# Layer 1's experts in a four-layer transformer kernel: from all experts for every token to routed blocks

## The chip, the cores and the metric

The kernel runs on one core of a Trainium2 chip. The metric is the device time of one execution in microseconds. Before the change the median of 3 runs is 2787.91 us (2787.64 to 2787.95). All matrix work is done by TensorE (PE in the profile); VectorE (DVE), ScalarE (ACT) and GpSimd (POOL) work on data in SBUF; TensorE's results stand in eight PSUM banks, which VectorE and ScalarE empty. The queue of SyncE (SP) issues almost all transfers.

## The reference, cut to what matters

The input is 16 sequences of 256 tokens, each a row of 128 numbers: 4096 tokens in 32 tiles of 128, or 8 chunks of 512. Four layers follow on each other. Each has an attention and a feed-forward part, whose results are scaled by gates (and whose inputs are normalized, scaled and shifted) by numbers that come from a conditioning vector through a SiLU. Layer 1's feed-forward part is itself a small transformer layer over groups of tokens, and its second half is the mixture of experts that the change is about:

```python
x1 = _ln(src + _attention(src, ...), ln1_g, ln1_b)      # 16 heads of 8
gates = softmax(xf @ gW + gb)                           # 8 experts
top2_scores, top2_idx = top_k(gates, 2)
w = (one_hot(top2_idx, 8) * top2_scores[..., None]).sum(1)
h = relu(einsum('nd,edf->enf', xf, W1) + b1[:, None, :])    # d 128, f 256
y = einsum('enf,efd->end', h, W2) + b2[:, None, :]
out = _ln(x1 + einsum('ne,end->nd', w, y), ln2_g, ln2_b)
```

Each token uses two of eight experts, with the softmax weights of all eight (not renormalized over the two). The result is multiplied by the layer's gate and added to the residual stream. Layer 0 has a mixture of experts of the same shape (8 experts, 2 per token, with two up products and a SiLU); layer 2 has 16 experts, layer 3 none. Layer 2's attention has 16 heads of 8 and is causal.

## The kernel before

**Stages.** The program is a list of nine stages: the wide attention of layer 0, its routed experts, the wide attention of layer 1, `narrow_attention(1)` (the attention inside layer 1's feed-forward part), `moe(1, 8)` (its experts), `narrow_attention(2)` (layer 2's attention), `moe(2, 16)`, and the two stages of layer 3. Each stage is written as a loop of ticks. Every engine has its own stream of instructions, written out by hand tick by tick and executed strictly in order; semaphores join the streams. A stage may lend its last ticks to the stage behind it: the `Guest` that a stage gives as its `start` is run there, from tick `guests_at` on, and a stage's last pieces (its tail) are run in the first ticks of the next stage. There is no planner: the place of a piece in the loop of ticks is its place in each queue.

**Layer 1's narrow attention** has 128 ticks of 1.9 us and a drain to tick 137. In a tick TensorE computes one pair of heads' scores twice, once as they are and once transposed, and the value product of an earlier tick. VectorE takes the row maxima of the scores from PSUM (`rowmax`, line 3015). GpSimd turns each group of them into two bf16 parts (`negate`, lines 2738 and 2740), TensorE transposes these (line 2965) and adds them to the transposed scores, and ScalarE exponentiates. For each of 16 pairs of tiles (8 ticks each) GpSimd also splits the queries and keys into three bf16 parts (`Parts.gpsimd`, lines 2664 to 2672), SP stores them to device memory (line 2686) and loads them back in the layout that the products want (line 2695). Before the change the stage's last 11 ticks host the first pieces of `moe(1, 8)` (`guests_at` is 126).

**Layer 1's experts**, `moe(1, 8)`, compute every expert for every token: 8 chunks of 512 tokens with 8 experts each are 64 steps. A step has two up products, weights of 128x128 by 512 tokens, two ReLUs on ScalarE, and a down part of eight 128x128 products; VectorE weights each expert's four result tiles by the token's gate and adds them to an accumulator (`vector_down`, line 2359). The gates come from TensorE's logits, ScalarE's exponential and VectorE's choice of two by comparison of all pairs (line 1153 and those behind it). When a chunk's eight experts are in, its own normalization follows (`gpsimd_finish`, lines 2488 to 2498, and its counterparts on VectorE): add to x1, statistics, a power on GpSimd (line 189), scale and shift, gate, add to the residual X (`gated`, `added`).

**Layer 0's routed experts** are the model for the change. Two of its chunks are computed densely, in the time in which the other six, 3072 tokens and so 6144 token-expert pairs, are routed. VectorE finds each token's two experts with `max` (line 1525) and `max_index` (line 1529); TensorE ranks the tokens within their expert with products of a mask; VectorE makes from that a table that assigns experts to 31 blocks of 256 rows (lines 1579 to 1587 and on). GpSimd scatters each tile's rows twice, once for each expert, to a buffer `hs` in device memory (line 1854, 48 indirect transfers). Then come 31 blocks: SP loads the block's rows (line 1891) and its expert's weights (line 1898), TensorE turns the rows (line 1432), computes the up and the down part on 256 rows, VectorE adds the second bias (line 1706) into one of two result buffers, and SP stores it to `ys` (line 1903). Their result is brought together during the wide attention of layer 1: GpSimd gathers a tile's two result rows (`late_fetch`, line 1209, two indirect transfers per tile of 128 tokens) and weights and adds them itself (`late_combine`).

**Layer 2's narrow attention** has the same ticks as layer 1's, with a causal mask. Its first step for a pair of tiles is the normalization of X for the chunk that the pair belongs to: `stats0` and `stats1` on VectorE, `normed0` and `normed1`, and `turn` on TensorE. These need the chunks of X that layer 1's experts have finished; the last chunk of the experts finishes in the first ticks, as the tail of the stage before.

## Time and profile before

| | |
|---|---|
| median of 3 runs | 2787.91 us |
| the profiled execution's own time | 2784.46 us |
| its span | 2782.7 us |
| mean granted TensorE clock | 0.984 |
| TensorE busy | 2608.1 us, 94% |
| VectorE busy | 2015.3 us, 72% |
| ScalarE busy | 1664.5 us, 60% |
| GpSimd busy | 1180.9 us, 42% |
| device memory traffic | 87 GB/s over the span |

The span is the time from the first to the last instruction that the profiler recorded; the execution's own time holds 1.8 us more. Times in rows are microseconds from the start of the span. The stretches that the change touches are: layer 1's narrow attention with ticks from about 1510, its tick 122 at 1742 and its drain to 1771; layer 1's experts from 1771 to 2031; layer 2's narrow attention, tick 0 at 2031, to about 2250 and on. Layer 0's blocks run from 777 to 889. A granted clock of 1.00 is TensorE's full clock of 2.4 GHz, 0.50 its lower level of 1.2 GHz.

### The profile page before, as it was taken

What the parts mean: (1) busy time and instruction counts of PE and PEld (TensorE: products, weight loads), DVE (VectorE), ACT (ScalarE), POOL (GpSimd) and SP (SyncE); (2) the same over time, 40 slices, a digit from 0 to 9 for tenths busy, and PEclk for the clock granted to TensorE, in tenths of its full rate; (3) what the DMA queues carried; (4) which work ended last, traced back from release to release, by engine and by line L of the source; (5) the groups of instructions that cost most, each with busy time, mean ns of one, the idle gap of its engine ahead of it and who ended that gap; (6) DMA issues with size and microseconds to landing.
All of it is one profiled execution on the core that took longest, in us unless ns stands there. A gap on an engine that the chain in (4) does not pass through costs nothing.

```text
span 2782.7 us, 67999 instructions
## 1 busy us (share of the span) xinstructions
PE 2608.1 (94%) x24870; PEld 1786.5 (64%) x24870; DVE 2015.3 (72%) x5620; ACT 1664.5 (60%) x4107; POOL 1180.9 (42%) x1620
## 2 busy tenths in 40 slices
PE   5999999998989999999997999999989988999898
PEld 2666666665677666666665555677767765666666
DVE  6888888876544666666666998556678886887675
ACT  3888888884334777677765777534335544434665
POOL 6888888862611566211113454122333321014441
PEclk9999999999999999999999999999989999999999
DMA  3022222112275122111113544000054433435750
GB/s 113 17 54 76 76 75 53 62 37 75 98 224 164 30 45 46 32 33 32 32 32 106 182 142 133 1 1 17 13 159 141 129 102 63 93 78 154 208 164 28
DMA packets 218858, 230.81 MB, mean 83 GB/s; under 512 B 18609, under 2 KB 188273, under 8 KB 216481
## 3 DMA queue, kind: packets, MB, share of 16 engines
q1 hardware_dynamic: 212000, 207.58, 26.9%
q10 hardware_dynamic: 3456, 12.58, 1.4%
q0 software_dynamic: 3072, 6.30, 0.8%
q8 instruction: 201, 3.29, 0.5%
q14 instruction: 129, 1.05, 0.1%
HBM read 165.87 MB, written 75.60 MB: 87 GB/s over the span
## 4 chain that ended last, share of the span: by engine, by line
PE 71%; DVE 13%; ACT 7%; issue 4%; POOL 2%; SPq 1%; DMA 1%; ACTq 0%; another core or an unknown queue 0%; DVEq 0%; POOLq 0%
PE pb L163 63%; ACT big L967 4%; PE pb L663 3%; ACT big L160 2%; DVE big L3015 2%; DVE big L837 2%; PE pb L596 1%; DVE big L236 1%; PE pb L2986 1%; SPq L2686 1%; DVE big L3520 1%; PE pb L249 1%; DVE big L820 1%; DVE big L179 1%; DVE big L842 1%
## 5 line engine op out<-in xcount | busy, mean ns | idle before, releaser
L163 PE MATMUL pb<-big 128*128 128x128 f32 (+12 forms) x19624 | 2344.0, 326 | 100.1 <-ACT big L160 32.6
L163 PEld LDWEIGHTS pb<-big 64*128 64x128 bf16 (+4 forms) x19624 | 1475.6, 143 | 756.5 <-issue 424.7
L160 ACT ACTIVATE big<-pb 128x512 f32<-128x512 f32 (+7 forms) x1481 | 846.1, 620 | 552.7 <-PE pb L163 292.6
L160 ACT ACTIVATE big<-pb,big 128x512 f32<-128x512 f32 (+2 forms) x502 | 276.3, 585 | 426.7 <-PE pb L163 360.1
L3015 DVE TENSOR_REDUCE big<-pb 128x4 f32<-128x1024 f32 (+1 forms) x256 | 277.6, 1086 | 69.5 <-PE pb L163 64.9
L967 ACT ACTIVATE big<-big 128x256 f32<-128x256 f32 x512 | 253.7, 499 | 65.8 <-DVE big L842 64.6
L967 ACT ACTIVATE big<-pb,big 128x128 f32<-128x128 f32 (+1 forms) x512 | 256.7, 526 | 60.0 <-DVE big L822 59.8
L837 DVE CUSTOM_DVE_ANT_0 big<-pb,big 128x256 f32<-128x256 f32 x512 | 186.7, 422 | 96.7 <-PE pb L163 93.5
L187 POOL TENSOR_SCALAR big<-big 128x4 f32<-128x4 f32 (+2 forms) x102 | 26.7, 262 | 535.6 <-DVE big L182 535.4
L174 POOL TENSOR_TENSOR big<-big 128x128 f32<-128x128 f32 x168 | 74.5, 457 | 348.8 <-DVE big L171 348.7
L1046 POOL TENSOR_TENSOR big<-big 128x512 f32<-128x512 f32 x128 | 159.7, 1273 | 140.7 <-DMA big<-recip 140.7
L663 PEld LDWEIGHTS pb<-big 64*128 64x128 f32 x3584 | 146.2, 139 | 75.0 <-ACT big L967 58.4
L663 PE MATMUL pb<-big 64*128 64x64 f32 x3584 | 158.3, 225 | 26.0 <-ACT big L967 25.0
L1020 POOL TENSOR_TENSOR big<-big 128x32 f32<-128x32 f32 x32 | 174.1, 5440 | 2.7
L747 DVE TENSOR_TENSOR big<-pb,big 128x512 f32<-128x512 f32 x256 | 164.0, 681 | 12.2 <-PE pb L163 10.9
L904 DVE COPY big<-pb 128x384 f32<-128x384 f32 (+1 forms) x256 | 157.3, 615 | 5.2 <-PE pb L663 4.3
L2359 DVE SCALAR_TENSOR_TENSOR big<-pb,big 128x128 f32<-128x128 f32 x256 | 72.0, 344 | 95.6 <-PE pb L163 95.6
L1011 POOL TENSOR_TENSOR big<-big 128x256 f32<-128x256 f32 x128 | 82.3, 643 | 86.0 <-DVE big L747 82.9
L596 PEld LDWEIGHTS pb<-big 128*128 128x128 f32 x512 | 63.6, 142 | 75.9 <-issue 66.1
L967 ACT ACTIVATION_READ_ACCUMULATOR big<-pb,big 128x1 f32 x512 | 111.1, 217 | 0.0
L236 DVE TENSOR_SCALAR big<-big 128x128 f32<-128x128 f32 x244 | 95.6, 444 | 8.5 <-POOL big L189 8.4
L2738 POOL CAST big<-big 128x16 bf16<-128x16 f32 x96 | 21.8, 227 | 188.2 <-DVE big L3019 73.5
(211 smaller groups left out, 2451.2 us busy)
## 6 DMA issues: line engine op xcount, KB each, us to landing
parts<-big SPq DMA_DIRECT2D x384, 96.0 KB, 2.5
big<-parts SPq DMA_DIRECT2D x72, 512.0 KB, 4.1
big<-recip SPq DMA_DIRECT2D x128, 256.0 KB, 5.3
big<-comb SPq DMA_DIRECT2D x32, 512.0 KB, 8.4
hs<-in_zero SPq DMA_DIRECT2D x10, 1472.0 KB, 8.8
big<-in_wx SPq DMA_DIRECT2D x31, 450.0 KB
parts<-big SPq DMA_DIRECT2D x192, 64.0 KB, 2.1
big<-parts ACTq DMA_DIRECT2D x24, 512.0 KB, 4.6
```

The lines of the kernel that those rows point to most:

```text
L160: return e.activation(o, i, f, bias=bias, scale=scale)
L163: return e.matmul(o, l, r_, start=start, stop=stop, skip_group_check=True)
L236: t = e.tensor_scalar(XN[:, i, :], X[:, self.tiles(c)[i], :], mv[:, k0 + i, 0:1], rs[:, k0 + i:k0 + i + 1], ALU.subtract, ALU.mult)
L596: t = e.transpose(bk[:, 128 * m:128 * m + 128], QR[(8 * b + n) % 12][:, 128 * m:128 * m + 128], IDF)
L663: t = e.transpose(banks[2 * (p % 2) + half][:, 64 * at:64 * at + 64], PS[p % 2][rows, i, 128 * blk:128 * blk + 128], IDF[rows, rows])
L747: t = e.tensor_tensor(h3(D), h3(bk), TAB[:, 2 * qk + kk, tile, :].unsqueeze(1).to_broadcast([128, 8, 64]), ALU.mult)
L837: t = e.tensor_tensor_reduce(ps[:, i, x], banks[2 * (p % 2) + i][:, x], U[:, 2 * j + i, 128 - 128 * qt:384 - 128 * qt], 1.0, -3.0e38, ALU. ...
L904: e.tensor_copy(*turned_out(t - 1, 0)).then_inc(even_out, 1)
L967: t = e.activation(ps, banks[2 * s + i][:, at:at + w] if causal else ps, ACT.Exp, bias=NM[s][:, m:m + 1], scale=rstd_q(b)[:, qt, h:h + 1] ...
L1020: e.tensor_tensor(half, half, HALF, ALU.pow).then_inc(rms_made, 1)
L1046: e.tensor_tensor(OT[k % 6], OT[k % 6], R[:, 2 * i:2 * i + 2, :], ALU.mult).then_inc(chunk_scaled, 1)
L3015: e.tensor_reduce(m[:, :, 0:n, jj], two[:, :, 0:width].rearrange("p e (q x) -> p e q x", q=n), AXX, ALU.max, negate=True).then_inc(maxed, 1)
```

## The change

`moe(1, 8)` is replaced by a new stage, `routed_ffn()`.

**Routing.** Six of the eight chunks (0 to 5) are routed. Their `turn` (transposition of x1), `logits`, `max0`, `max1`, `route`, `rank`, `place` and the three pieces of the table are hosted in layer 1's narrow attention, whose `guests_at` goes from 126 to 34; one tick there has at most one or two of them. GpSimd scatters from tick 58 on: one indirect transfer a tick in ticks 58 to 73 and 90 to 105, two a tick from 122 to 129.

**Blocks.** The new stage begins with 31 blocks of 256 rows, one a tick, with one up product of 256 columns for each half of f, a ReLU for each half, and a down part of eight 128x128 products (two halves of f for two tiles of rows, each product issued as two instructions). Weights are 128 x 642 f32 a block (329 KB), rows 128 x 256 f32 (131 KB), results the same.

**Dense.** Chunks 6 and 7 are computed as before, 16 steps, behind the blocks. Their logits, gates and first accumulator values are made beside the blocks, as are the shares (softmax weights) and the places of the result rows (`home`) of the routed ones, and the modulation numbers of the next layer.

**Combination.** The 24 routed tiles' result rows are gathered by GpSimd in 12 groups m of two tiles, four indirect transfers each, into three buffers `CHOSEN1`. VectorE, not GpSimd as in layer 0, weights them and adds them to x1, eight operations for a chunk of four tiles, and makes the statistics; GpSimd makes the scale, ScalarE normalizes, and GpSimd does the rest with 256-wide operations and issues the next gathers in the same piece of its order. Chunks 0 and 1 are brought together at ticks TB+4, TB+5 and TB+9, TB+10 (TB is 31, where the dense steps begin); chunks 2 to 5 in the ticks 0 to 3, 10 to 13, 26 to 29 and 42 to 45 of layer 2's narrow attention.

**Layer 2's narrow attention** waits for the routed chunks by a semaphore of their own (`arrived`), takes its statistics one to three ticks later (offsets 5 and 6 in place of 2 and 4), opens with 9 hosted steps in place of 7, and the transfer of the second gates goes from pair 5 to pair 11. The semaphores that engines use to wait for themselves are one per engine in place of one per stage. The host lays out the layer's weights once more, by expert (`wx1`).

```diff
@@ narrow_attention
-            guests_at = 126 if k == 1 else 98
+            guests_at = 34 if k == 1 else 98
...
-                                                           ((2, "stats0"), (4, "stats1"))) if at == i]
+                                                           (((5, "stats0"), (6, "stats1")) if causal else ((2, "stats0"), (4, "stats1")))) if at == i]
...
+            def late_at(t):
+                found = []
+                for c in range(2, 6) if causal else ():
+                    first = 16 * (c - 2) - (6 if c > 2 else 0)
+                    found += [(c, p) for p, at in (("scale", 0), ("sum", 1), ("stats", 2), ("norm", 3)) if first + at == t]
+                return found
...
+                        for c, p in late_at(t):
+                            if p == "norm":
+                                late_ffn_finish(e, c)
@@ the stages
-                 moe(1, 8, X1A.rearrange("p (t c) -> p t c", c=128)), narrow_attention(2), moe(2, 16), layer3_attention(), layer3_mix()]
+                 routed_ffn(), narrow_attention(2), moe(2, 16), layer3_attention(), layer3_mix()]
@@ new functions
+        def late_ffn_fetch(e, m):
...
+            if m >= 3:
+                e.wait_ge(ffn_added, m - 2)
+            for k in range(2):
+                for i in range(2):
...
+                    e.indirect_dma_start(out=CHOSEN1[m % 3][:, k, i, :], out_offset=None, in_=dr["ys"],
+                                         in_offset=bass.IndirectOffsetOnAxis(ap=at, axis=0)).then_inc(chosen_in[m % 3], 16)
...
+        def late_ffn_vector(e, c):
...
+            for a, t in tiles:
+                x = e.scalar_tensor_tensor(out=a[:, 0, :], in0=a[:, 0, :], scalar=SHARE1[:, 0, t:t + 1], in1=X1[:, t, :],
+                                           op0=ALU.mult, op1=ALU.add)
...
+            for a, t in tiles:
+                x = e.scalar_tensor_tensor(out=a[:, 0, :], in0=a[:, 1, :], scalar=SHARE1[:, 1, t:t + 1], in1=a[:, 0, :],
+                                           op0=ALU.mult, op1=ALU.add)
...
+        def late_ffn_finish(e, c):
+            own = gpsimd_own
+            e.wait_ge(ffn_mean, c + 1)
...
+            e.tensor_tensor(LRS, LRS, EPS[:, 0:4], ALU.pow).then_inc(own.sem, own.up())
+            e.wait_ge(own.sem, own.n)
+            e.tensor_tensor(LNMR, LNMR, LRS, ALU.mult).then_inc(ffn_rstd, 1)
+            e.wait_ge(ffn_normed, c + 1)
...
+            for m in (2 * c, 2 * c + 1):
+                a = CHOSEN1[m % 3][:, 0]
+                for b, op in ((two(LNW[:, 256:384]), ALU.mult), (two(LNW[:, 384:512]), ALU.add), (two(GA[:, m, 128:256]), ALU.mult)):
+                    e.tensor_tensor(a, a, b, op).then_inc(own.sem, own.up())
+                    e.wait_ge(own.sem, own.n)
+                e.tensor_tensor(X[:, 2 * m:2 * m + 2, :], X[:, 2 * m:2 * m + 2, :], a, ALU.add).then_inc(ffn_added, 1)
+            for m in (2 * c + 3, 2 * c + 4):
+                if m < 12:
+                    late_ffn_fetch(e, m)
@@ routed_ffn
+            FIRST_TICK = 34
+            def hosted_at(t):
+                found = []
+                for c in ROUTED:
+                    b = 16 * c + FIRST_TICK
+                    found += [(c, p) for p, at in (("turn", 0), ("logits", 2), ("max0", 3), ("max1", 4)) if b + at == t]
+                    if c % 2:
+                        found += [("ABC"[c // 2], p) for p, at in (("route", 5), ("rank", 6), ("place", 6)) if b + at == t]
+                        if c == 5:
+                            found += [("C", p) for p, at in (("table_a", 7), ("table_b", 8), ("table_c", 9)) if b + at == t]
+                return found
...
+            def tensor_block_up(e, j):
...
+                for f in range(2):
+                    t = mm(e, bk[:, 256 * f:256 * f + 256], WB[J % 4][:, 128 * f:128 * f + 128], HTB[J % 3], True, True)
...
+            def vector_block_down(e, j):
...
+                e.wait_ge(y_stored[J % 2], 16 * (J // 2))
+                e.tensor_tensor(YB[J % 2], bk[:, 0:256].rearrange("p (k c) -> p k c", k=2),
+                                WB[J % 4][:, 514:642].unsqueeze(1).to_broadcast([128, 2, 128]), ALU.add).then_inc(y.free, 1)
...
+            def gpsimd(e):
+                for t in range(T + 2):
...
+                    if t == TB + 1:
+                        for m in range(3):
+                            late_ffn_fetch(e, m)
+                    if late_at(t):
+                        late_ffn_gpsimd(e, *late_at(t))
+                    if t >= TB + 9:
+                        gpsimd_finish(e, *finish_at(t))
...
+                    if j + 3 < TB:
+                        sync_rows(e, j + 3)
+                    if 1 <= j and j + 3 < TB:
+                        sync_weights(e, j + 3)
+                    if j >= 1:
+                        sync_store(e, j - 1)
```

## Rows read from the trace of the kernel before

**Rows 1.** The page: busy time, chain by engine, one costly group.

```profile
PE 2608.1 (94%) x24870; PEld 1786.5 (64%) x24870; DVE 2015.3 (72%) x5620; ACT 1664.5 (60%) x4107; POOL 1180.9 (42%) x1620
...
PE 71%; DVE 13%; ACT 7%; issue 4%; POOL 2%; SPq 1%; DMA 1%; ACTq 0%; another core or an unknown queue 0%; DVEq 0%; POOLq 0%
...
L1011 POOL TENSOR_TENSOR big<-big 128x256 f32<-128x256 f32 x128 | 82.3, 643 | 86.0 <-DVE big L747 82.9
```

**Rows 2.** Stretches: us, busy PE, PEld, DVE, ACT, POOL, clock, DMA share, GB/s.

```profile
1550.00:1740.00 190.00, 184.42 (x2202) 101.53 (x2196) 174.93 (x344) 135.96 (x185) 97.61 (x208) 1.00 0.46 142
1740.00:1771.00 31.00, 26.68 (x309) 14.71 (x306) 19.42 (x48) 19.73 (x27) 8.97 (x25) 1.00 0.00 1
1771.00:2031.00 260.00, 257.25 (x1526) 191.35 (x1524) 153.63 (x538) 98.62 (x151) 62.49 (x105) 0.99 0.06 17
2031.00:2053.00 22.00, 15.17 (x148) 9.27 (x150) 17.36 (x43) 2.82 (x4) 12.34 (x22) 0.69 0.38 118
2053.00:2250.00 197.00, 193.11 (x3022) 141.10 (x3020) 159.17 (x321) 107.85 (x169) 68.63 (x130) 1.00 0.47 143
```

**Rows 3.** Waits, 1550 to 1740: who waited for whom, us, times, longest.

```profile
PEld pb L163 <- DVE big L3015: 30.1, 75, 1.0
...
DVE big L3015 <- PE pb L163: 7.1, 20, 0.6
```

**Rows 4.** TensorE's groups by shape, 1780 to 2000: count, busy us, mean ns.

```profile
L163 PE MATMUL pb<-big 128*128 128x128 f32 x907 | 110.5, 275 | 0.0
L163 PE MATMUL pb<-big 128*128 128x512 f32 x224 | 106.7, 599 | 0.0
```

**Rows 5.** Timeline of a layer-0 block: start, duration, instruction, idle before.

```profile
844.09 0.84 ACT L160 ACTIVATE big<-pb,big 128x256 f32<-128x256 f32 x2 [1.37 <-PE pb L163]
...
844.50 0.43 SPq L1903 DMA_DIRECT2D ys<-big  x1
...
844.75 0.38 PE L1432 MATMUL pb<-big 128*128 128x128 f32 x2
...
845.17 0.39 ACT L160 ACTIVATE big<-pb 128x256 f32<-128x256 f32 x1 [0.24 <-PE pb L1432]
...
846.06 0.43 DVE L1706 TENSOR_TENSOR big<-pb,big 128x256 f32<-128x256 f32 x1 [0.18 <-PE pb L163]
...
847.59 0.38 PE L1432 MATMUL pb<-big 128*128 128x128 f32 x2
```

**Rows 6.** A stretch of layer-0 blocks, columns as in rows 2.

```profile
846.00:856.00 10.00, 10.00 (x63) 9.02 (x62) 4.33 (x10) 4.23 (x11) 0.00 (x0) 1.00 0.92 250
```

**Rows 7.** Transfers by kind: count, KB each, median us from issue to landing.

```profile
ys<-big SPq DMA_DIRECT2D x31, 128.0 KB, 4.3
```

**Rows 8.** Timeline of GpSimd, two gathers of layer 0's result rows.

```profile
893.80 0.95 POOL L1209 DMA_INDIRECT big<-ys,big  x1 [0.30 <-issue]
895.07 0.94 POOL L1209 DMA_INDIRECT big<-ys,big  x1 [0.30 <-issue]
```

**Rows 9.** GpSimd's groups by shape, 1780 to 2040: the power.

```profile
L189 POOL TENSOR_TENSOR big<-big 128x4 f32<-128x4 f32 x10 | 10.5, 1050 | 0.8
```

**Rows 10.** Timeline of VectorE, routing pieces of layer 0.

```profile
651.66 0.36 DVE L1525 MAX8 big<-big 128x8 f32<-128x8 f32 x4
...
652.55 0.16 DVE L1529 FIND_INDEX8 big<-big 128x8 uint32<-128x8 f32 x1
...
752.59 0.22 DVE L1587 TENSOR_REDUCE big<-big 128x8 f32<-128x64 f32 x1
```

**Rows 11.** Timeline of TensorE, start of layer 2's narrow attention.

```profile
2042.38 0.40 PE L2965 MATMUL pb<-big 128*128 128x128 bf16 x2 [1.14 <-POOL big L2740]
```

**Rows 12.** A stretch soon after that opening, columns as in rows 2.

```profile
2044.00:2048.00 4.00, 1.96 (x20) 1.43 (x20) 3.00 (x6) 0.00 (x0) 3.63 (x7) 0.50 0.05 14
```

**Rows 13.** VectorE's groups by shape, 1780 to 2000: two comparisons of gates.

```profile
L1155 DVE TENSOR_TENSOR big<-big 128x256 f32<-128x256 f32 x7 | 8.3, 1189 | 0.0
...
L1153 DVE TENSOR_TENSOR big<-big 128x256 f32<-128x256 f32 x7 | 3.0, 427 | 0.2
```

More of the change, by code:

```diff
@@ L1196, in program @@
         NBLK, SLOT_ROWS = 31, 3072
+        place(21632)
+        HOME1 = [alloc(16).bitcast(U32) for _ in range(3)]
+        SHARE1 = alloc(48).rearrange("p (k m) -> p k m", k=2)
+        CHOSEN1 = [WA[:, a:a + 512].rearrange("p (k i c) -> p k i c", k=2, i=2) for a in (2176, 2688, 3200)]
+        LST = WA[:, 3840:3864].rearrange("p (i s) -> p i s", i=4)
+        LMV = WA[:, 3864:3872].rearrange("p (i s) -> p i s", i=4)
+        LRS, LNMR = WA[:, 3872:3876], WA[:, 3876:3880]
         def late_fetch(e, n):
@@ L1238, in routed_experts @@
             T = TD + NBLK
-            own, own_g = moe_own
-            scattered, marked, spaced, share_exped = sem("scattered"), sem("marked"), sem("spaced"), sem("share_exped")
-            placed, table_made = sem("placed"), sem("table_made")
-            rows_in = [sem(f"rows_in{i}") for i in range(3)]
-            weights_in = [sem(f"weights_in{i}") for i in range(4)]
+            own, own_g = vector_own, gpsimd_own
             some = lambda n: [alloc(512) for _ in range(n)]
@@ L2751, in narrow_attention @@
             place(stack_top)
-            own, own_g = narrow_own
+            own, own_g = vector_own, gpsimd_own
             causal = k == 2
@@ L3281, in tail_do @@
                 return go
-            start = Guest(15 if k == 1 else 7, lambda i: [take_piece(b, piece, BK[6:8]) for b, piece in hosted_step(i)],
+            start = Guest(15 if k == 1 else 9, lambda i: [take_piece(b, piece, BK[6:8]) for b, piece in hosted_step(i)],
                           tensor_hosted, vector_hosted, scalar_hosted, gpsimd_hosted, sync_hosted)
@@ L3314, in layer3_attention @@
             place(20480)
-            own, own_g = narrow_own
+            own, own_g = vector_own, gpsimd_own
             bi = WI[:, 512:643]
```

677 lines of the change are left out of this document (658 added, 19 removed).

## The prediction

> **What bounds the kernel now.** I read the page first: TensorE is busy for 94% of the span and holds 71% of the chain that ended last [rows 1]. The table by stretches then cuts out the part that the change touches [rows 2]. Four things are to be seen there. In layer 1's dense experts (1771 to 2031 us) TensorE is busy 257 of 260 us, VectorE 154, GpSimd 62: TensorE alone bounds it. In layer 1's attention (1550 to 1740) VectorE is busy 175 of 190 us. Its waits [rows 3] say that TensorE waited 30.1 us for VectorE's row maxima, and VectorE only 7.1 us for TensorE: VectorE bounds this stage, though TensorE looks busy. In layer 2's attention (2053 to 2250) TensorE leads again, VectorE has 19% free and GpSimd 65%. And the first 22 us of that stage are a stretch of waits, at a mean granted clock of 0.69.
>
> **Part 1, the dense stage that goes: minus 260 us.** 64 expert steps of two 128x512 products and eight 128x128 ones; the rows show 224 and 907 instructions in 220 us, so each product is two instructions [rows 4]. By shares of that stretch a step takes about 3.44 us and a chunk 31 us with gates.
>
> **Part 2, the 31 blocks: 86 us.** Layer 0's blocks in this trace are the model; one lasts 2.84 us (847.59 less 844.75) [rows 5]. A layer-1 block has one up product fewer: 4 instructions of 0.213 us (0.85), a down part of 8 by 0.107 (0.86) and the row turn 0.22, so TensorE wants 1.93 us. ScalarE gives more: the block's activations start 0.25 us after the up part, take 0.84, and the copy of the next rows, queued behind them, 0.39, before the next up part may start: 0.85 + 0.25 + 0.84 + 0.39 + 0.1 = 2.43 us. DMA: weights 329 KB, rows 131, results 131 make 591 KB a block; at layer 0's 250 GB/s [rows 6] that is 2.36 us. The result buffers close a third loop: writing a result (0.43), 0.85 us until SP has issued the weights before it and then the store, landing 4.3 us in the median [rows 7], two buffers. With 132 KB less ahead of the store I take 3.8 us: (0.43 + 0.85 + 3.8) / 2 = 2.55 us. Ends: 2.43 and 2.95 us; I take 2.55, 79 us in all. Beside them: two table loads for Silu, the 1 MB gate broadcast, two gates of about 3.6 us on VectorE, two chunks' turns: 7 us (3 to 14). At the start, the last 16 scatters are queued two a tick from tick 122 of the attention: 16 x 1.26 us [rows 8] and 5 us of other GpSimd work end some 25 us later, the drain of the attention takes 29; scatter landing, row load and copy leave 2 us of TensorE waiting (0 to 8).
>
> **Part 3, the dense rest and GpSimd's queue: 85 us.** Two chunks cost an up part beside the last block's down part (2.6), an up part (1.7), 14 steps of 3.44 and two down parts (3.4), 56 us, and the first pieces of layer 2's attention 5: 61 us if nothing waits. But the gathers are issued here: four for two tiles, 1.26 us each (893.80 to 895.07) [rows 8], 24 tiles, so 60 us of GpSimd for all 48 in place of nothing. Count from the first dense up part. The last result lands and GpSimd starts at 6; twelve gathers end at 21. VectorE weights and adds (eight operations at a 0.28 us pitch, statistics 1.3: 3.8 us) by 22; GpSimd's scale needs 1.6 with the power of 1.05 [rows 9], ScalarE 1.7, GpSimd's eight 128x256 operations at 0.64 [rows 1] 5.8 us: 31; then, in the same piece of its order, eight gathers, 41. Chunk 1's turn repeats it to 64. Only behind that stands the scale of the first dense chunk (65), for which VectorE waits at tick 42 with evacuations behind it; VectorE's normalization also came late, so TensorE's turn at tick 42 waits 8 us. TensorE's next piece, v of pair 0, needs a bank that VectorE empties at about 72. I get 16 us more there, and a late split and return trip of pair 0, so that the next stage starts at 85 in place of 61. Ends: 61, if the order costs nothing, and 97.
>
> **Part 4, routing in layer 1's attention: plus 24 us.** Per pair of chunks VectorE gets eight MAX8 and eight index searches, whose pitch in the timeline is 0.09 and 0.13 us (the first MAX8 of a half at 651.66, its last index search at 652.55) [rows 10]: 2.4 us in four halves; route 1.3, place 1.0, logits 0.3; three pairs are 15 us, the three table pieces 3.4 (some thirteen operations at a pitch of 0.26, such as the one at 752.59) [rows 10]: 18.4 us. An engine that is late by nothing for most ticks pays this in full. TensorE's logits and rank products delay its next scores by some 7 us more; 2 us of VectorE's idle time absorb part. I take 24. Ends: 9, if all 8% of idle time is used, and 38. Scatters there are 1.26 us a tick on a GpSimd at half load [rows 2, 8]; with negated maxima due three ticks later I count nothing for them, 4 us if that cover is gone.
>
> **Part 5, layer 2's attention: plus 52 us.** Here each late chunk stops three engines in turn. VectorE's 3.8 us stand between two row maxima; ScalarE's normalization waits in order for GpSimd's scale, and the exponentials behind it wait: 4.3 us a chunk. Then GpSimd has 5.8 us of arithmetic and up to eight gathers (10.1 us) before the split of the next pair (3.5) and the next negated maxima, for which TensorE waits within three ticks (6 us). For chunk 2 (tick 3) this meets the opening: before, TensorE got its first negated maxima at 2042.38 [rows 11], 11.4 us after tick 0 at 2031; now the dense rest's scaling (14 us), 1.6 + 1.7 + 5.8 and 10.1 put it at 33.7: plus 22. Chunk 3: split and maxima end 28.5 us after its tick, needed at 18.2: 10 + 4.3 = 15. Chunk 4 has four gathers: 5 + 4.3 = 10. Chunk 5 none: 5. Sum 52. Ends: 17 (only the 4.3 us each) and 72: TensorE's clock stood at 0.50, its lower level of 1.2 GHz, at 2044 to 2048 after such waiting [rows 12], and at 1.00 from 2053 on [rows 2]; four more such stretches at 4 us each, and one late return of a pair.
>
> At this point the trace and a page differ in weight. Beside GpSimd's work, VectorE's 128x256 comparison of two SBUF operands took 1189 ns on average where its twin took 427 [rows 13]. The Trainium skill, "SBUF — State Buffer", section "Who interferes with whom", says that a VectorE instruction with two SBUF inputs contends with a GpSimd instruction that reads SBUF and is held until it ends. Sixteen of the new weight-and-add operations run while gathers are being issued; if each were held for one, by that rule, they would cost about 12 us more than the sum has, and the kernel would end near 2789.
>
> **The sum.** minus 260 + 86 + 2 + 85 + 24 + 52 = minus 11 us. The profiled execution took 2784.5 us (span 2782.7), the median run 2787.9, 3.4 more: 2773 for a profiled one, 2777 us for the median.
>
> **Rivals.**
> A. GpSimd's queue hides: casts and splits are late by less than their slack. Rows 2 speak for it (GpSimd 24% busy in the dense stage, 35% in layer 2's attention), the 10 to 16 us pieces in its order against it. Part 3 then gives 66 and part 5 26: minus 56, 2732 to 2750, I say 2745 with some of the stalls left.
> B. The order decides, and slower: each gather piece of 10 us in layer 2's attention also delays the split of the next pair, whose return trip then stops the scores at the pair's first tick, and TensorE runs the ticks after each stop at 1.2 GHz. Place: ticks 3 to 40 there; price 20 us on part 5 and 12 on part 3; it turns the change slower once the stops of parts 3 and 5 exceed 87 us (260 less 86, 2, 61 and 24), against the 76 in my sum. 2808.
> C. The port of rows 13: as in the paragraph above, the held VectorE operations take 0.76 us more each (1189 less 427), sixteen of them: 12 us, so minus 11 becomes plus 1, 2789.
> D. The blocks are bound by DMA at 2.95 us: 12 us more, 2789 as well.
>
> **Chances.** Forecast 0.38 (own range 2767 to 2789), A 0.27, B 0.22, C 0.07, D 0.06. Less than 0.2% (5.6 us) is no change that a measurement of this kernel tells: 2782.3 to 2793.5. Faster: A and two thirds of the forecast, 0.52; the same: most of C and D and a fifth of the forecast, 0.18; slower: B and the rest, 0.30. The range that leaves out two in ten, into A and B: 2742 to 2812.
>
> **What would show it.** Right: blocks at 2.4 to 2.7 us with ScalarE busy 1.2 of them; GpSimd without a gap from the first gather to the scale of the first dense chunk; VectorE waiting for GpSimd's power some 15 us; TensorE's wait for negated maxima near 20 us at the start of layer 2's attention and again some 35 us later; layer 1's attention 20 to 28 us longer. Wrong: no TensorE wait above 3 us between the last block and the end of layer 2's attention (A); or stops that also name the returning pairs (B). The forecast fails as a whole if routing costs under 10 us in layer 1's attention, since then VectorE did not bound it.

## The result, and the profile after

The changed kernel takes 2833.59 us in the median of 4 runs (2828.06 to 2842.45), the kernel before 2787.93 (4 runs): ratio 1.0175, 95% interval 1.0157 to 1.0193. It is 46 us slower. Forecast were 2777 us, range 2742 to 2812. The profiled execution has a span of 2834.7 us, 52.0 more than before.

The page of the changed kernel, parts 1 and 4, beside [rows 1]:

```profile
PE 2535.8 (89%) x24300; PEld 1731.3 (61%) x24300; DVE 1955.7 (69%) x5508; ACT 1642.7 (58%) x4123; POOL 1277.5 (45%) x1716
...
PE 62%; DVE 15%; ACT 7%; issue 6%; POOL 4%; DMA 3%; SPq 2%; another core or an unknown queue 0%; ACTq 0%; DVEq 0%; POOLq 0%
```

TensorE, VectorE and ScalarE have less to do, the span is longer: TensorE's share of the chain went from 71% to 62%. The time is in waits. The next table says where, with the columns of [rows 2]. The stretches are layer 1's attention, its drain, the blocks, the dense rest with the first pieces of layer 2's attention, and that attention in three parts.

```profile
1512.00:1801.00 289.00, 243.04 (x2752) 138.97 (x2752) 231.28 (x527) 164.88 (x225) 156.76 (x280) 0.96 0.43 133
1801.00:1822.00 21.00, 14.68 (x161) 6.50 (x156) 5.94 (x20) 11.25 (x14) 14.21 (x25) 0.92 0.20 65
1822.00:1912.00 90.00, 76.73 (x493) 64.54 (x493) 29.55 (x96) 38.45 (x100) 3.57 (x9) 0.96 0.72 194
1912.00:2007.00 95.00, 72.80 (x382) 52.77 (x384) 40.81 (x160) 27.48 (x46) 58.82 (x79) 0.87 0.18 54
2007.00:2041.00 34.00, 7.46 (x66) 4.02 (x61) 15.15 (x46) 1.65 (x4) 19.20 (x28) 0.60 0.24 78
2041.00:2140.00 99.00, 75.15 (x993) 51.80 (x994) 56.41 (x132) 39.03 (x62) 49.88 (x83) 0.83 0.35 111
2140.00:2362.00 222.00, 190.72 (x2810) 135.07 (x2806) 160.18 (x389) 102.71 (x165) 67.92 (x130) 0.93 0.38 111
```

In layer 1's attention TensorE is busy for 243 of 289 us; before, from 1510 to 1752, it was 226 of 242. So it has some 17 us more to do there, as much as VectorE (231 us, before 215). Between 2007 and 2041 it works for 7.5 us of 34.

Each tick of both attentions has one row maxima instruction (`rowmax`), so that the times of the 256 of them cut the whole kernel. From these starts in the timelines, in us:

| | first maxima | attention 1 | between | attention 2 | rest | span |
|---|---|---|---|---|---|---|
| before | 1509.5 | 242.2 | 279.3 | 277.3 | 474.4 | 2782.7 |
| changed | 1512.5 | 288.7 | 205.9 | 355.4 | 472.2 | 2834.7 |
| difference | +3.0 | +46.5 | -73.4 | +78.1 | -2.2 | +52.0 |
| forecast | 0 | +24 | -87 | +52 | 0 | -11 |

What follows are the places behind these differences, all of the changed kernel.

**Layer 1's attention, tick 120.** VectorE's and TensorE's rows in the timeline:

```profile
1778.86 1.21 DVE L3815 TENSOR_REDUCE big<-pb 128x4 f32<-128x1024 f32 x1
...
1781.07 0.17 DVE L2371 TENSOR_TENSOR big<-big 128x8 bf16<-128x8 bf16 x1
1781.29 1.18 PE L163 MATMUL pb<-big 128*128 128x64 bf16 x20 [1.71 <-DVE big L2371]
1782.08 1.23 DVE L3815 TENSOR_REDUCE big<-pb 128x4 f32<-128x1024 f32 x1 [0.85 <-PE pb L163]
```

TensorE's `rank` (a 128x64 bf16 product) waits for the end of VectorE's `route` (L2371), which VectorE runs behind the row maxima of the same tick; then VectorE waits for TensorE's next scores. Each engine in turn is idle for the other, in strict order.

**The dense rest.** VectorE's normalization of the first dense chunk, and TensorE's v product of layer 2:

```profile
1981.90 1.12 DVE L2511 TENSOR_SCALAR big<-big 128x128 f32<-128x128 f32 x4 [18.18 <-issue]
...
1987.64 15.78 PE L163 MATMUL pb<-big 128*128 128x128 f32 x88 [12.72 <-DVE big L3840]
```

GpSimd's power for the scale of L2511 ran only from 1980.8 to 1981.9, behind chunk 1's arithmetic and its eight gathers; VectorE stood 18.2 us in front of it, and TensorE 12.7 us in front of VectorE.

**The opening of layer 2's attention**, GpSimd's rows from the end of chunk 2's arithmetic, and TensorE's:

```profile
2029.83 0.72 POOL L2044 TENSOR_TENSOR big<-big 128x256 f32<-128x256 f32 x1
2030.72 1.11 POOL L1982 DMA_INDIRECT big<-ys,big  x1 [0.16 <-POOL big L2044]
...
2039.64 0.95 POOL L1982 DMA_INDIRECT big<-ys,big  x1 [0.31 <-issue]
2040.60 0.23 POOL L3524 CAST big<-big 128x16 bf16<-128x16 f32 x1
...
2041.20 0.39 PE L3765 MATMUL pb<-big 128*128 128x128 bf16 x2 [20.60 <-POOL big L3526]
```

TensorE got its first negated maxima 34.1 us after tick 0 at 2007.1 (before 11.4 us, [rows 11]; forecast 33.7), 20.6 us of it in one wait, whose last 10 us are the eight gathers (2030.7 to 2040.6).

**Chunk 4, tick 29 there**, a stop that the forecast had smaller:

```profile
2111.26 0.87 POOL L174 TENSOR_TENSOR big<-big 128x128 f32<-128x128 f32 x2 [8.62 <-DVE big L171]
...
2113.89 0.20 POOL L2036 TENSOR_TENSOR big<-big 128x4 f32<-128x4 f32 x1
2114.13 1.65 ACT L160 ACTIVATE big<-big 128x128 f32<-128x128 f32 x4 [7.93 <-POOL big L2036]
...
2116.52 1.25 PE L163 MATMUL pb<-big 64*128 64x256 bf16 x12 [5.12 <-ACT big L160]
```

ScalarE's normalization waits 7.9 us for the scale (L2036). GpSimd is not busy then: it stands in front of the attention's residual step (L174), which is ahead of the scale in its order and waits for VectorE, which in turn has 3.6 us of the chunk's weighting and statistics (2105.8 to 2109.4) and a row maxima in front of it.

**Tick 87 to 96 there**, a loss that the forecast did not have:

```profile
2261.05 1.04 POOL L189 TENSOR_TENSOR big<-big 128x4 f32<-128x4 f32 x1
2262.05 0.61 POOL L3450 CAST big<-big 128x512 bf16<-128x512 f32 x1
...
2278.55 4.50 PE L163 MATMUL pb<-big 64*128 64x256 bf16 x56 [2.12 <-DMA big<-parts]
```

The statistics that were moved to offsets 5 and 6 put the power (L189) right in front of the split of the next pair (L3450); its trip through device memory ends late, and TensorE waits 2.1 us at tick 96.

### The profile page after: what moved, and what is told of

Same layout as the page of the kernel before. It is cut to its first block, busy times and chain, and to the rows that moved or that the text cites. A ratio compares the mean times of both kernels' runs of the same rounds, so it can differ in the third digit from the quotient of the medians.

```text
span 2834.7 us, 67087 instructions
## 1 busy us (share of the span) xinstructions
PE 2535.8 (89%) x24300; PEld 1731.3 (61%) x24300; DVE 1955.7 (69%) x5508; ACT 1642.7 (58%) x4123; POOL 1277.5 (45%) x1716
## 4 chain that ended last, share of the span: by engine, by line
PE 62%; DVE 15%; ACT 7%; issue 6%; POOL 4%; DMA 3%; SPq 2%; another core or an unknown queue 0%; ACTq 0%; DVEq 0%; POOLq 0%
PE pb L163 54%; ACT big L966 4%; PE pb L662 3%; DVE big L3815 3%; ACT big L160 3%; DVE big L836 2%; PE pb L595 1%; SPq L3472 1%; DMA big<-hs 1%; DVE big L236 1%; DVE big L4330 1%; DMA big<-parts 1%; PE pb L3786 1%; DVE big L179 1%; POOL big L1982 1%
## 5 line engine op out<-in xcount | busy, mean ns | idle before, releaser
L163 PE MATMUL pb<-big 64*128 64x256 bf16 (+13 forms) x19016 | 2262.5, 329 | 178.5 <-DVE big L3815 52.4
L163 PEld LDWEIGHTS pb<-big 128*128 128x128 f32 (+4 forms) x19016 | 1412.7, 143 | 808.1 <-issue 405.2
L160 ACT ACTIVATE big<-pb 128x512 f32<-128x512 f32 (+7 forms) x1512 | 857.6, 615 | 616.8 <-PE pb L163 327.5
L160 ACT ACTIVATE big<-pb,big 128x256 f32<-128x256 f32 (+2 forms) x468 | 236.0, 549 | 383.4 <-PE pb L163 305.0
L3815 DVE TENSOR_REDUCE big<-pb 128x4 f32<-128x1024 f32 (+1 forms) x256 | 277.7, 1087 | 150.7 <-PE pb L163 130.7
L174 POOL TENSOR_TENSOR big<-big 128x128 f32<-128x128 f32 x144 | 64.3, 458 | 367.4 <-DVE big L171 367.3
L966 ACT ACTIVATION_READ_ACCUMULATOR big<-big 128x1 f32 x512 | 96.1, 188 | 0.0
```

The lines of the kernel that those rows point to most:

```text
L160: return e.activation(o, i, f, bias=bias, scale=scale)
L163: return e.matmul(o, l, r_, start=start, stop=stop, skip_group_check=True)
L966: t = e.activation(ps, banks[2 * s + i][:, at:at + w] if causal else ps, ACT.Exp, bias=NM[s][:, m:m + 1], scale=rstd_q(b)[:, qt, h:h + 1] ...
L3815: e.tensor_reduce(m[:, :, 0:n, jj], two[:, :, 0:width].rearrange("p e (q x) -> p e q x", q=n), AXX, ALU.max, negate=True).then_inc(maxed, 1)
```

## The experiments

All are edits of the changed kernel. Jobs ran on other chips than the first result; there the kernel before took 2778 to 2782 us and the changed one 2816, so totals are compared within a job, and stretches through the same row maxima. In these jobs, nine kernels whose code in layer 1's attention is unedited gave 279.5 to 281.0 us there, 8 less than the first profile (288.7). Kernels whose code in a stretch is unedited spread from 203.9 to 210.4 us between the attentions and from 351.5 to 354.5 in layer 2's (355.4 in the first profile); a smaller difference tells nothing. no_scatters, max_twice, stats_early, gathers_spread, third_y, rows_ahead_third_y and dense_order ran once each.

**after_again**: no edit.

> The changed kernel once more, beside the others on one chip, since its first profile had an attention of layer 1 that was 8 us longer than two kernels with the same code there. Theory: what is fixed in the order (each tick's pitch outside DMA waits) repeats to 0.1 us; total 2815 to 2830 us, with layer 1's attention at 280 to 289 and layer 2's at 353 to 356 us between first and last row maxima.

Measured 2816.46 us (2814.6 to 2820.8), ratio 1.0130 (1.0113 to 1.0147); attentions 280.4 and 351.8 us, between them 205.1. The pitches of most ticks repeat to 0.1 us. The yardsticks below are 280.4, 205.1 and 351.8.

**max_twice**: VectorE's searches in layer 1's attention are done twice.

```diff
+                for again in range(2):
+                    if again:
+                        e.wait_ge(own.sem, own.n)
+                    for t in tiles:
+                        x = e.max(MX8[:, t, :], LG[:, t, :])
...
```

> Each half of the MAX8 and index searches of layer 1's routing is done twice (same result), some 0.6 us of VectorE's work more in each of twelve ticks, 7 us in all. Theory B (VectorE bounds every tick, each us of its work is paid): the attention's maxima go from 288.7 to 296 us. Theory A (the ticks are held by round trips with TensorE; VectorE has idle time in most of these ticks now): 288.7 to 292 us.

Attention 289.7 us, 9.3 more than 280.4. The second search starts 0.67 us behind the first (1591.16 and 1591.83), so that twelve add 8 us, not 7; in eleven of the twelve ticks the time from one row maxima to the next grew by 0.7 us, and 1.1 more fell on each of ticks 53 and 121. So this work is paid one for one, as theory B says (both theories were reckoned from 288.7, the longer first profile). It is the second search in the tick that is: the first ones, 1.35 us of a chunk, had lengthened their two ticks by 0.8 us. And this although VectorE waits for TensorE for 31.6 us in 245 us of that attention in after_again, where it was 7.1 in 190 [rows 3].

**route_moved**: the same pieces in other ticks.

```diff
-                    found += [(c, p) for p, at in (("turn", 0), ("logits", 2), ("max0", 3), ("max1", 4)) if b + at == t]
+                    turn, logits, rank = (3, 4 if c == 0 else 5, 9) if c < 5 else (1, 2, 6)
+                    found += [(c, p) for p, at in (("turn", turn), ("logits", logits), ("max0", logits), ("max1", logits + 1)) if b + at == t]
...
-                        found += [("ABC"[c // 2], p) for p, at in (("route", 5), ("rank", 6), ("place", 6)) if b + at == t]
+                        found += [("ABC"[c // 2], p) for p, at in (("route", logits + 2), ("rank", rank), ("place", rank)) if b + at == t]
...
-                    per, first = (1, 32 * g + 58) if g < 2 else (2, 122)
+                    per, first = (1, 32 * g + 61) if g < 2 else (2, 122)
```

> Only the ticks of the hosted routing pieces in layer 1's attention change: turn, logits, maxima, route and rank/place stand at offsets 3, 5, 5/6, 7, 9 of a chunk in place of 0, 2, 3/4, 5, 6 (the last chunk at 1, 2, 2/3, 4, 6, the first chunk's logits at 4), scatters 3 ticks later for the first two groups. Work is the same. Theory A (round trips in order: TensorE's turn stands where its bank is emptied by VectorE behind that tick's row maxima, TensorE's rank waits for VectorE's route of the same tick): from the first to the last row maxima of the stage 275 us in place of 288.7 (before: 242.2), total 12 to 18 us less than 2833.6. Theory B (VectorE's added work is paid in full, wherever it stands): 286 to 289 us, total unchanged within 3 us.

Attention 273.6 us, total 2812.87 (ratio 1.0114, 1.0090 to 1.0138). Against 280.4, the yardstick, placement is worth 7 us. Theory A, reckoned from 288.7, asked for 14 us there: both theories hold in part. Of the 38 us by which this attention is longer than before (242.2), 31 are left.

**no_scatters**: the first 32 of the 48 scatters are left out.

```diff
-                    if 0 <= t - first < 16 // per:
+                    if g == 2 and 0 <= t - first < 16 // per:
```

> The first two groups' 32 scatters in layer 1's attention are left out (those tokens' expert results are then not computed from their rows; the last 16 scatters stay), all else as in the changed kernel. Theory A (the scatters have no price: GpSimd has time): attention of layer 1 280 us between its first and last row maxima, as in the kernels with the same code. Rival (they make the negated maxima and x1 late, so that TensorE stops at the maxima and at the turn): 272 to 277 us.

Attention 276.7 us: 32 scatters cost 3.7 us there, not nothing (2.9 to 4.4 against the nine kernels), at the upper end of the rival's 272 to 277 us.

**stats_early**: the statistics back at offsets 2 and 4, from the second chunk on.

```diff
-                                                           (((5, "stats0"), (6, "stats1")) if causal else ((2, "stats0"), (4, "stats1")))) if at == i]
+                                                           (((5, "stats0"), (6, "stats1")) if causal and c == 2 else ((2, "stats0"), (4, "stats1")))) if at == i]
```

> In layer 2's attention the statistics of the next chunk go back to offsets 2 and 4 of a chunk, as in the kernel before, but for the first one. Theory: at offsets 5 and 6 GpSimd's power (1.3 us with its add) stands right ahead of the split of the next pair, whose return trip then ends 2 to 3 us late at ticks 63, 79, 95 and 112: these ticks go back to the pitch of before, the stage's maxima from 355.4 to 346 us. Rival (the late return comes from DMA traffic or from the lower clock): no change of those ticks, 355 us.

Attention 2 took 347.0 us, 4 to 8 less than the 351.5 to 355.4 of kernels with the same code there. From tick 56 to tick 112 it took 124.9 us, as before (124.8), where after_again took 131.0 and the other kernels with the late power 129.6 to 135.4. The late power is the cause of that loss.

**scale_first**: GpSimd's scale at the head of the tick, the rest one tick later.

```diff
+                    for c, p in late_at(t):
+                        if p == "norm":
+                            late_ffn_scale(e, c)
                     if tail_at(t) >= 0:
                         tail.gpsimd(e, tail_at(t))
...
-                    for c, p in late_at(t):
+                    for c, p in late_at(t - 1):
                         if p == "norm":
-                            late_ffn_finish(e, c)
+                            late_ffn_rest(e, c)
```

> In layer 2's attention alone GpSimd makes a late chunk's scale at the start of its tick, ahead of the tick's other pieces, and ScalarE's normalization and GpSimd's rest stand one tick later. Work and gathers are the same. Theory A (ScalarE waits in order for a scale that GpSimd has behind a residual step that itself waits for VectorE's next tick, 7.9 us a chunk): the stage's maxima span 355.4 us now; chunks 4 and 5 lose 8 us each, chunk 3 some 2 us, 337 us. Rival (GpSimd's arithmetic and gathers behind the scale decide): 350 to 356 us, as the stops move to the split of the next pair.

343.5 us, 8 less where theory A wanted 18. The pitches (us from one row maxima to the next) tell why:

| tick | before | changed (after_again) | scale_first | gathers_spread | attn2_all |
|---|---|---|---|---|---|
| 6 | 4.0 | 22.6 | 19.1 | 13.9 | 6.1 |
| 15 | 2.1 | 6.3 | 3.0 | 6.3 | 4.1 |
| 19 | 2.3 | 12.7 | 15.5 | 3.1 | 2.8 |
| 31 | 1.9 | 8.5 | 1.7 | 8.5 | 2.5 |
| 35 | 2.2 | 7.5 | 11.5 | 3.1 | 3.9 |
| 47 | 1.9 | 8.1 | 1.7 | 8.4 | 2.9 |
| 51 | 2.2 | 2.2 | 5.6 | 2.2 | 3.8 |

The stops at 31 and 47 are gone, and four ticks later, where TensorE needs negated maxima, new ones stand: GpSimd's arithmetic and gathers had been hidden behind the stop that was removed.

**gathers_spread**: the finish stays, its gathers go out one a tick.

```diff
-                    for c, p in late_at(t):
-                        if p == "norm":
-                            late_ffn_finish(e, c)
+                    for back in range(9):
+                        for c, p in late_at(t - back):
+                            if p == "norm" and not back:
+                                late_ffn_scale(e, c)
+                                late_ffn_rest(e, c, fetch=False)
+                            elif p == "norm" and 2 * c + 3 + (back - 1) // 4 < 12:
+                                late_ffn_fetch(e, 2 * c + 3 + (back - 1) // 4, [(back - 1) % 4])
```

> In layer 2's attention the finish of a late chunk stays where it is and whole, only its gathers go out one a tick behind it instead of eight (four) at once. Theory: of the stops at the first split and negated maxima behind each finish, 10 us of the opening's 20 and 10 of the 10.4 at tick 19 are the eight gathers, 5 of the 5.3 at tick 35 the four; stage maxima from 352 to 328 us. Rival (the arithmetic and the waits for VectorE and ScalarE make them): above 342 us.

333.1 us, 18.7 less. Tick 6 lost 8.7 us, tick 19 9.6, tick 35 4.4: that is eight, eight and four gathers of 1.26 us, almost one for one. The attention as a whole gained less than these 22.7 us; tick 11 got 1.9 longer, for one. Ticks 31 and 47 stay, which are ScalarE's waits. The two stops are two causes.

**attn2_all**: both, the arithmetic in two halves, and the statistics early.

```diff
+                    for back in range(1, 11):
+                        for c, p in late_at(t - back):
+                            if p == "norm" and back < 3:
+                                late_ffn_rest(e, c, (back - 1,), False)
+                            elif p == "norm" and 2 * c + 3 + (back - 3) // 4 < 12:
+                                late_ffn_fetch(e, 2 * c + 3 + (back - 3) // 4, [(back - 3) % 4])
```

> Layer 2's attention: scale at the start of the tick, normalization one tick later, GpSimd's arithmetic for the two tile pairs one and two ticks later, and its gathers one a tick behind that, no longer eight or four at once; statistics of the next chunk at offsets 2 and 4 as in the kernel before (first chunk 6 and 7). Same work. Theory A (only the order on GpSimd makes the stops; left is VectorE's 3.8 us a chunk and the opening): stage maxima from 354 to 310 us: minus 6 each at ticks 15 to 23 and 31 to 35, 12 at tick 19, 6 to 8 at tick 47, 7 at the late statistics, some 8 of the opening's 20. Rival (GpSimd has too much work there, in any order): 335 to 345 us, as when the scale alone was put first and the stop went from tick 31 to tick 35.

303.4 us for the attention, 48.4 less, with the same instructions; theory A asked for 310. Of what is left over the kernel before (26 us), 11 are on ticks 3, 13, 29 and 45, where VectorE weights and adds a chunk's rows. The whole takes 2769.24 us (2765.82 to 2773.31), ratio 0.9966 (0.9953 to 0.9979): this reordering of one stage turns the change from 1.3% slower to 0.3% faster than before. TensorE's first negated maxima there, for the 20.60 of the changed kernel:

```profile
2006.72 0.40 PE L3776 MATMUL pb<-big 128*128 128x128 bf16 x2 [1.09 <-POOL big L3537]
```

**dense_gathers** and **dense_order**: in the dense rest, chunk 1's eight gathers one a tick from dense tick 11; then also chunk 1's arithmetic behind the short pieces.

```diff
+                    if late_at(t) == (1, "norm"):
+                        late_ffn_scale(e, 1)
...
                     if 0 <= t - guests_at < guest.steps:
                         guest.gpsimd(e, t - guests_at)
+                    if late_at(t) == (1, "norm"):
+                        late_ffn_rest(e, 1, fetch=False)
+                    for n in {11: (0,), 12: (1,), 13: (2,), 14: (3, 4), 15: (5,), 16: (6,), 17: (7,)}.get(t - TB, ()):
+                        late_ffn_fetch(e, 5 + n // 4, [n % 4])
```

> In the new stage the eight gathers behind chunk 1 are no longer issued at once: one a tick from dense tick 11 on, behind the first dense chunk's normalization. Same work. Theory: TensorE's stop of 12.7 us (its v product waits for a bank that VectorE empties behind its 18.2 us wait for that normalization's scale) goes, the gap between the two attentions from 206 to 194 us; the gathers that are put off may lengthen the opening of layer 2's attention by up to 3 us. Rival (GpSimd is busy from the first gather to the end of the stage, so that the order changes nothing but the place): 203 to 206 us.

> Chunk 1's gathers spread as in the kernel before this one, and its arithmetic (5.8 us of GpSimd) behind the scale of the first dense chunk and of the next layer's normalization. Theory: TensorE's waits of 7.6 us (turn of the next layer's first chunk) and 4.9 us (its v product) for VectorE fall to 3 us in sum, gap from 198 to 189 us. Rival: 196 to 199, GpSimd's sum decides.

The stretch between the attentions went from 205.1 to 198.2 us (2810.34 us in all, ratio 1.0115, 1.0098 to 1.0132) and then to 192.8, each some 4 us short of what its theory asked (194 and 189): 12 of the 24 us of stalls that Part 3 of the prediction had were order alone.

**third_y** and **rows_ahead_third_y**: a third result buffer for the blocks; then also the rows of block j+4 ahead of the store of block j-1 in SP's queue.

```diff
-            YB = [alloc(256).rearrange("p (k c) -> p k c", k=2) for _ in range(2)]
+            YB = [alloc(256).rearrange("p (k c) -> p k c", k=2) for _ in range(3)]
...
-                    if j + 3 < TB:
-                        sync_rows(e, j + 3)
+                    if j == 0:
+                        sync_rows(e, 3)
+                    if j + 4 < TB:
+                        sync_rows(e, j + 4)
```

> The 31 blocks get a third result buffer. Theory A (the loop of result buffers holds a block, 2.96 us on average where a block without waits takes 2.34): VectorE's waits for stores, 11.5 us, go, gap between the two attentions 206 to 197 us. Rival (rows and weights come late on a busy DMA, 18 us of TensorE's waits for rows): the waits move to the rows, gap within 2 us of 206.

> The blocks get the third result buffer, and SP issues the rows of block j+4 ahead of the store of block j-1, one block earlier than now. Theory A (the third buffer alone moved the wait to the rows, since these stand in SP's queue behind a store that waits for VectorE): TensorE's waits for rows, 21 us with the third buffer, fall below 6; blocks at 2.5 us in place of 2.93, gap between the attentions 205 to 193 us. Rival (DMA is busy, each landing is late by as much): 203 to 206 us.

TensorE's row turn (62 products), what its idle time ended by, with the third buffer and then with rows ahead as well. These rows add the waits before products (7.9 and 1.7 us) to those before weight loads (12.7 and 2.2), and the two overlap:

```profile
L2237 PE MATMUL pb<-big x62: 272/273/476, 1810.7 to 1899.4; 128*128 128x128 f32 x62
its engine sat idle before it (us, times) until:
  DMA big<-hs: 20.7, 18
```

```profile
L2237 PE MATMUL pb<-big x62: 272/273/421, 1799.5 to 1887.9; 128*128 128x128 f32 x62
its engine sat idle before it (us, times) until:
  DMA big<-hs: 3.9, 2
```

The third buffer took 12.5 us of VectorE's waits for stores away and the stretch fell by 1.5 us only, to 203.6. TensorE's products had waited for rows for 7.1 us in after_again and wait for 7.9 now: that wait stayed. Rows ahead took most of it away as well, and the 31 blocks still last 88.4 us (88.7 with the third buffer alone), 203.8 between the attentions: two waits of TensorE's products, 6.9 us in sum, whose releaser the trace does not name, take its place. One of them, 5.5 us to 1885.8, stands where SP had issued the 1 MB gate broadcast at 1874.8 and the next weights behind it; the broadcast landed 9.7 us later, and from 1876 to 1880 the DMA engines were busy throughout. That the block waited for its weights behind the broadcast is likely and was not tested. Both theories A fail in size; these edits alone gain nothing, which is what the rivals said.

**all2** and **all2_again**: route_moved, attn2_all, dense_order, third_y and rows ahead together.

> All the orders together: routing pieces moved in layer 1's attention, rows ahead and a third result buffer in the blocks, dense stage's gathers and arithmetic behind the short pieces, layer 2's attention reordered. The work of the changed kernel, instruction for instruction. Theory A (order, not work, made it slower): 2816 less 7, 12, 16 and 49 us = 2732 us, some 1.6% under the kernel before on this chip. If the gains overlap (GpSimd's work put off from the dense stage meets the opening of layer 2's attention): 2745 us.

> The kernel with all orders once more, to see whether its lead over the kernel before repeats, since one of its five runs took 11104 us: 2738 to 2750 us, ratio 0.985 to 0.990, and no such run again if it was the chip's.

2745.04 us, ratio 0.9874 (0.9853 to 0.9896), and again 2748.88, ratio 0.9885 (0.9865 to 0.9906). One of the first job's five executions took 11104 us; it is in the median and not in the interval, the second job's five had none like it, and its cause stays open. The profile of all2, over layer 1's attention, the stretch between, and layer 2's attention:

```profile
1501.00:1774.00 273.00, 239.47 (x2750) 137.41 (x2746) 232.19 (x527) 165.41 (x225) 156.30 (x280) 0.97 0.46 138
1774.00:1961.00 187.00, 157.92 (x1028) 121.27 (x1026) 77.90 (x275) 76.50 (x160) 76.36 (x113) 0.96 0.47 129
1961.00:2267.00 306.00, 263.74 (x3889) 187.42 (x3886) 237.68 (x567) 143.26 (x231) 138.59 (x240) 0.93 0.43 127
```

The two are 71 and 68 us under after_again, in other jobs; by their own traces layer 1's attention gained 7 us, the stretch between 18 and 15, layer 2's attention 47 and 46. That is what the parts gained alone (7 + 48 + 12 + 1) within the spreads named above; of the 84 us of the first case 16 were to come from the blocks, and did not. The 2745 us of the second case came true for another reason than it gave: layer 2's attention took 305 us here and 303.4 alone, so that the gains hardly overlap.

## Why the prediction was wrong

The sign was wrong: minus 11 was forecast, plus 46 (profiled plus 52) measured. The mechanisms of Parts 3 and 5 were right and their sizes too small; in Part 4 the pieces of TensorE were priced too low, and what they wait for was left out. Of the 63 us between the forecast and the profiled difference Part 5 has 26, Part 4 22 and Part 3 10.

**Part 1** (minus 260) and the start (2 us: the drain took 20.7 us from the last maxima to the first block's rows, 19 before): held.

**Part 2**, 86 us: 90. A block without a wait takes 2.33 us (2.43 forecast as the end of ScalarE's loop), but the 31 took 2.96 on average, with the pieces beside them. VectorE's waits for stores (11.5 us) and TensorE's for rows (7.4 us before its products, 10.6 before its weight loads, which overlap) are in it. The longest of these, 4.9 us to 1906.8, ends where the 1 MB gate broadcast has landed (issued at 1897.8, 8.6 us); the rows that TensorE waits for were issued behind it (a likely cause, not tested). Rival D had the number (2.95). Its cause is not shown: DMA was busy for 72% over the blocks, and full beside the broadcast (a share of 1.04 from 1904 to 1907); two edits moved waits and left the length, and what bounds the blocks as a whole stays open.

**Part 3**, 85 us: 95. The mechanism stood as told: GpSimd without a pause above 1.8 us from the first gather at 1921 to the dense chunk's scale at 1981, VectorE waiting 18 us for it.

**Part 4**, 24 us: 46 in the first profile, 38 in the others. This is one of the two steps that failed. It took VectorE's 18.4 us once, plus 7 for TensorE's logits and rank products, less 2 that idle time absorbs. VectorE's term was about right: its busy time in this attention rose by 17.1 us (214.8 to 231.9 in after_again). TensorE's rose by 15.5 (226.1 to 241.6, a part of it the lower granted clock, 0.96 for 1.00), twice the term. The pitches of after_again, less those of the kernel before, say where the 38 us are:

| ticks | forecast | longer by, us |
|---|---|---|
| the six turns, and the tick behind each | 0 | 8.3 |
| the six logits | 7, with rank | 7.0 |
| the tick behind the logits | 0 | 6.4 |
| the twelve of searches, VectorE | 18.4 in all | 5.5 |
| route and rank, place, table, VectorE | | 11.3 |

All other ticks together are 0.3 us shorter. So 22 us stand in ticks in which VectorE has at most 0.16 us more to do. The turns had no term. A chunk's eight logits products hold TensorE for 1.03 us, and VectorE waits for the scores behind them (L3815 at 1582.76). One tick later TensorE's next product waits for a bank that VectorE empties (L2318, the logits) behind its maxima and statistics, and VectorE's next maxima come late for it. VectorE's rows in after_again, ticks 36 and 53:

```profile
1580.74 0.48 DVE L3831 TENSOR_SCALAR big<-pb,big 128x256 f32<-128x256 f32 x1
1582.76 1.23 DVE L3815 TENSOR_REDUCE big<-pb 128x4 f32<-128x1024 f32 x1 [1.54 <-PE pb L163]
...
1618.19 0.16 DVE L2318 TENSOR_TENSOR big<-pb,big 128x32 f32<-128x32 f32 x1
1619.99 1.23 DVE L3815 TENSOR_REDUCE big<-pb 128x4 f32<-128x1024 f32 x1 [1.65 <-PE pb L163]
```

Two causes inside these 38 us were tested. route_moved shows 7 us of placement: VectorE runs the pieces of tick t behind the maxima of tick t+1, while TensorE runs them in tick t, so that a piece of TensorE one tick behind its input on VectorE stops both. And 32 of the 48 scatters, costed at nothing because GpSimd was half idle, took 3.7. The rest is read from the pitches, not tested by an edit. The 8 us by which the first profile is longer lie on a few ticks, 4.4 of them on 121 to 125; their cause stays open, as the other nine don't have them.

**Part 5**, 52 us: 78. This is the other step that failed. By the pitches of after_again, whose attention is 74.5 us longer than before: opening 21 (22 forecast), chunk 3 19 (15), chunk 4 15 (10), chunk 5 11 (5), and 8 behind it, of which 6 to tick 112 are the statistics, an edit that the prediction never costed. The term that was too small is the 4.3 us a chunk: in chunks 4 and 5 it was 9, 2.5 at the tick where VectorE weights and adds (29, 45) and 6.4 on average two ticks later (31, 47), where ScalarE's stop was 7.9 us, since the residual step ahead of the scale was left out of GpSimd's queue. scale_first takes the stops at 31 and 47 away and so shows it.

**Rivals.** B was the nearest (2808 us). Its condition, stops of Parts 3 and 5 above 87 us, was met: 34 (95 less 61) and 78. Its place was right too, ticks 3 to 47 of layer 2's attention; but the late returns of pairs were only a tenth of it, the lower clock little (the tick behind each of the stops at 6, 15, 19, 31, 35 and 47 is at most 0.9 us longer than before), and Part 4 came on top. A failed. C failed by the trace: chunk 1's four weight-and-add operations, run while gathers were issued, and chunk 4's, run while GpSimd stood idle, take the same time.

```profile
1952.70 0.95 POOL L1982 DMA_INDIRECT big<-ys,big  x1 [0.31 <-issue]
1952.75 1.14 DVE L2005 SCALAR_TENSOR_TENSOR big<-big 128x128 f32<-128x128 f32 x4 [0.68 <-DMA big<-ys,big]
...
2105.81 1.13 DVE L2005 SCALAR_TENSOR_TENSOR big<-big 128x128 f32<-128x128 f32 x4
```

The Trainium skill, "SBUF — State Buffer", section "Who interferes with whom", has DMA on ports of its own; the equal times (1.14 and 1.13 us) fit that.

## What to carry to other kernels

Where several engines run hand-ordered streams, price a moved piece not by its busy time but by what stands ahead of it in its queue and what that waits for: here the same work took 2816 us in one order and 2745 to 2749 in another (with a third result buffer, which gained nothing by itself). Do so for each engine that gets a piece: here the tick of a piece on TensorE was lengthened at least as much as that of one on VectorE, and a piece on one engine also waits for a bank that the other empties late. Short pieces for which another engine waits (a scale, a power, a split) go ahead of long ones, and gathers go out one at a time. After a stop is removed, look for the next instruction of the engine that had used it as cover: one stop out of two or three hides another, so try the edits together as well as alone.

## What was not expected of the hardware

An indirect gather or scatter of 128 rows holds GpSimd's queue for 1.25 us, of which 0.95 is busy (the first of a row 1.4 and 1.1), in each stage that has them; twenty of them spread over ticks gave back 22.7 us on ticks 6, 19 and 35 in gathers_spread, 18.7 in the attention as a whole. After stops TensorE's clock did not stay at 2.4 GHz: the mean granted clock was 0.60 in the stretch from 2007 to 2041 and 0.93 from 2140 to 2362, where it was 1.00 before [rows 2].
